# An AdaLN attention block: first row opened by halves, and no barrier between the qkv rows and the spectral products

## The reference

```python
mod = (_silu(L0_c) @ L0_wmod).reshape(L0_c.shape[0], 6, 1, -1)
sa, ca, ga, sb, cb, gb = (mod[:, 0], mod[:, 1], mod[:, 2], mod[:, 3], mod[:, 4], mod[:, 5])
...
h = _layernorm(x, axis=-1) * (1 + ca) + sa
...
q = jnp.einsum('bld,ed->bel', u, Wq) + bq[None, :, None]      # k, v alike; u is h
...
kk_f = jnp.fft.rfft(ssm_k_kernel, n=n, axis=-1)               # 512 taps for each channel
k_f = jnp.fft.rfft(k, n=n, axis=-1)
shift_k = jnp.fft.irfft(kk_f * k_f, n=n, axis=-1)[..., :l]
k = shift_k + ssm_k_D[:, None] * k
```

## Time and profile before

| | us |
|---|---|
| three runs, median | 1235.82 |
| lowest, highest | 1230.43, 1235.84 |
| the profiled execution, its own time | 1234.52 |
| its span, first to last instruction | 1232.7 |
| TensorE busy in the span | 1127.4 (91%) |
| VectorE busy | 820.3 (67%) |
| ScalarE, GpSimd busy | 420.3 (34%), 546.8 (44%) |

### The profile page before, as it was taken

The page is one execution under the profiler, slowest core; times in us unless marked ns, Lnnn a source line. Parts: engine busy times, 40 slices in busy tenths (PEclk is TensorE's granted clock), DMA queues, the critical chain, the costliest instruction groups (busy, mean ns, idle before and its releaser), DMA issues.

```text
span 1232.7 us, 16948 instructions
## 1 busy us (share of the span) xinstructions
PE 1127.4 (91%) x5744; PEld 978.5 (79%) x5744; DVE 820.3 (67%) x1543; ACT 420.3 (34%) x760; POOL 546.8 (44%) x404
## 2 busy tenths in 40 slices
PE   6899998679999999999896548999999999999996
PEld 5788887468888888888785437889898989898996
DVE  3665999679999999999656776554444445444443
ACT  3430222023333333332554212344434434344432
POOL 2330000077777777775000004476565666575623
PEclk9999999789999999999985557999999999999999
DMA  7200021154111010112431213653544444434322
GB/s 260 69 1 1 2 50 43 37 171 134 32 32 32 32 32 32 32 32 68 130 110 40 89 52 87 188 147 61 138 70 133 86 116 82 122 79 73 64 45 26
DMA packets 69361, 93.35 MB, mean 76 GB/s; under 512 B 5652, under 2 KB 57620, under 8 KB 69320
## 3 DMA queue, kind: packets, MB, share of 16 engines
q1 hardware_dynamic: 51304, 60.96, 15.6%
q0 software_dynamic: 18016, 31.86, 13.1%
HBM read 65.29 MB, written 23.31 MB: 72 GB/s over the span
## 4 chain that ended last, share of the span: by engine, by line
PE 78%; DVE 15%; issue 2%; ACT 2%; POOL 1%; DMA 1%; DVEq 0%; SPq 0%; POOLq 0%
PE ps L1305 27%; PE ps L1444 18%; PE ps L1460 12%; DVE arena L371 6%; PE ps L1461 6%; PE ps L1228 5%; PE ps L1333 2%; PE ps L1426 1%; DVE arena L1042 1%; PE ps L1354 1%; DVE arena L380 1%; PE ps L1406 1%; DVE arena L361 1%; DVE arena L362 1%; DVE arena_rounded L797 1%
## 5 line engine op out<-in xcount | busy, mean ns | idle before, releaser
L1444 PE MATMUL ps<-arena_rounded,w_high 128*128 128x384 f32 (+1 forms) x768 | 211.5, 356 | 2.1 <-DVE arena_rounded L797 2.1
L569 POOL TENSOR_TENSOR kv_low<-arena,kv_high 128x512 fp32r<-128x512 f32 x128 | 187.0, 1490 | 38.7 <-ACT kv_high L621 38.7
L1305 PE MATMUL ps<-kv_high,toep_high 128*128 128x512 f32 (+1 forms) x512 | 193.9, 379 | 11.1 <-POOL kv_low L569 11.1
L1305 PE MATMUL ps<-kv_low,toep_high 128*128 128x512 f32 (+1 forms) x512 | 194.0, 379 | 0.0
L1305 PE MATMUL ps<-kv_high,toep_low 128*128 128x512 f32 (+1 forms) x512 | 193.1, 377 | 0.0
L1159 DVE SCALAR_TENSOR_TENSOR hidden_low<-ps,hidden_high 128x384 fp32r<-128x384 f32 (+1 forms) x192 | 115.5, 602 | 99.6 <-ACT hidden_high L766 99.1
L593 POOL DMA_INDIRECT out<-arena x80 | 126.3, 1579 | 104.2 <-DVE arena L797 96.7
L582 POOL DMA_INDIRECT qkv<-row_scratch,arena x80 | 82.7, 1033 | 188.4 <-DVE arena L1113 162.3
L1444 PEld LDWEIGHTS ps<-arena_rounded,w_high 128*128 128x128 f32 x768 | 140.9, 190 | 13.1 <-issue 2.5
L797 DVE TENSOR_TENSOR arena<-qkv 128x512 f32 (+1 forms) x128 | 136.8, 1126 | 12.6 <-SPq L335 12.6
L766 ACT ACTIVATE hidden_high<-ps 128x384 fp32r<-128x384 f32 (+1 forms) x192 | 101.3, 528 | 126.8 <-PE ps L1444 126.8
(11 more groups left out here) (176 smaller groups left out, 1958.7 us busy)
## 6 DMA issues: line engine op xcount, KB each, us to landing
arena<-ssm_scratch SPq DMA_DIRECT2D x32, 320.0 KB, 3.2
arena<-in_u SPq DMA_DIRECT2D x8, 1024.0 KB, 6.5
qkv<-in_w SPq DMA_DIRECT2D x16, 512.0 KB, 5.0
qkv<-in_w SPq DMA_DIRECT2D x8, 1024.0 KB, 9.2
row_scratch<-qkv SPq DMA_DIRECT2D x4, 1056.0 KB, 4.6
qkv<-arena SPq DMA_DIRECT2D x16, 256.0 KB, 3.5
row_scratch<-arena SPq DMA_DIRECT2D x4, 1024.0 KB, 6.3
out<-qkv SPq DMA_DIRECT2D x4, 1024.0 KB, 9.5
```

Source lines behind the costliest of these rows:

```text
L569: nc.gpsimd.tensor_tensor(kv_parts[s][1][:, quarter], kv_flat[s][:, quarter], kv_parts[s][0][:, quarter].bitcast(F32), ALU.subtract).then_ ...
L1305: last = mm(ps[:, 4 * s + g, (lo - 2 * g) * B * 64:BANK], toep_parts[s][a][:, o * P:(o + 1) * P], kv_parts[s][x][:, src], start=n == 0 and ...
L1444: last = mm(ps[:, f % 4, 0:width], w1_parts[q][a][:, dc * F + f * P:dc * F + (f + 1) * P], xeT_parts[x][dc][:, 0:width], start=dc == 0 and ...
```

## The change

**The opening.** SP loads row 0 of x in two halves, ahead of wmod, and wmod in two pieces: the parts that row 0's layernorm needs (`wmod_a`, 512 of 1536 columns) and, last, the rest (`wmod_b`). w_qkv, the second row, and the bias now come ahead of the taps and `dft`; `idft` is loaded after the late modulation. TensorE begins with five matmuls of zeros that nobody reads; ScalarE loads the table of its square root early, by an `activation` whose result is not read. Row 0 is normalized, transposed and opened by halves: TensorE makes tile 0 of row 0 before it transposes the second half. The taps' spectrum moves behind row 0's tiles, the rest of the modulation behind row 1's. One of the two low parts of w_qkv moves from GpSimd to VectorE. VectorE's two clamps now both stand in row 2.

**No barrier behind qkv.** `stage_end(0)` is gone on all engines. `forward(0)` stands behind row 2's tiles, `forward(1)` between the halves of row 3, `forward(2)` behind row 3. VectorE's products of unit 0 lie between the evacuations of row 3, those of unit 1 partly so. For this the regions are laid out anew: the spectra of the units alternate between two buffers, folded results too (before, the odd ones had four places), and `folded_product` waits from unit 2 on for the whole inverse of unit u - 2. The first Toeplitz loads wait for the last fold instead of the last join.

Unit 0's operations now stand between the evacuations, one group after each. The diff's core:

```diff
-            for dc in range(DC):
-                sp.dma_start(wmod_sb[dc], wmod[dc * P:(dc + 1) * P, :]).then_inc(wmod_in, 16)
-            sp.dma_start(x_buf[0], u_tiles[0]).then_inc(x_in[0], 16)
+            sp.dma_start(x_buf[0][:, 0:TB // 2], u_tiles[0][:, 0:TB // 2]).then_inc(x_half_in, 16)
+            sp.dma_start(x_buf[0][:, TB // 2:TB], u_tiles[0][:, TB // 2:TB]).then_inc(x_in[0], 16)
+            wmod_rows = wmod.rearrange("(c p) n -> p c n", p=P)
+            sp.dma_start(wmod_a, wmod_rows[:, :, 0:2 * D]).then_inc(wmod_in, 16)
             sp.dma_start(ident[:], K["ident"]).then_inc(ident_in, 16)
+            sp.dma_start(wqkvT, w_qkv.rearrange("(c p) n -> p c n", p=P)).then_inc(w_qkv_in, 16)
...
-                if unit >= 2 and parity == 0:
-
-
-                    dve.wait_ge(conv_psum, CT * (unit - 2) + CT // 2)
...
+            if unit >= 2:
+
+
+                dve.wait_ge(conv_psum, CT * (unit - 1))
...
-            for b in range(B):
+            for b in range(B - 1):
                 qkv_out(b)
                 if b + 2 < B:
                     finish_stats(b + 2)
+                if b == 1:
+                    taps_joined()
             dve.sem_inc(mod_ready, 1)
-            stage_end(dve, 0)
...
+            qkv_rows(B - 1, 0)
+            joined_spectrum(dve, link, 0)
+            qkv_rows(B - 1, 1)
+            turned_half(link)
+            qkv_rows(B - 1, 2)
+            real_products(link, 0)
+            qkv_rows(B - 1, 3)
+            real_difference(link)
+            imaginary_products(link, 0)
+            imaginary_sum(link)
+            folded_product(dve, link, 0)
+            qkv_rows(B - 1, 4)
+            qkv_rows(B - 1, 5)
+            joined_spectrum(dve, link, 1)
+            qkv_rows(B - 1, 6)
+            turned_half(link)
+            qkv_rows(B - 1, 7)
+            real_products(link, 1)
...
+            pe.wait_ge(idle_set, 1)
+            for _ in range(5):
+                mm(ps[:, 7, :], idle[:, 0:P], idle, start=True, stop=True)
             pe.wait_ge(siluT_ready, 1)
...
+            modulation_columns(0, wmod_a, SA * D)
+            modulation_columns(2, wmod_a, CA * D).then_inc(modT_psum, 1)
...
+            def late_modulation():
+                pe.wait_ge(wmod_late_in, 16)
+                pe.wait_ge(h_full_ready, 12)
+                modulation_columns(1, wmod_b, (SB - GA) * D)
+                modulation_columns(3, wmod_b, (CB - GA) * D).then_inc(modT_psum, 1)
...
             def forward(unit):
                 b = unit // 2
+                pe.wait_ge(qkv_ready, TB * (b + 1))
+                pe.wait_ge(h_full_ready, 4 * B)
...
-            for unit in range(3):
-                forward(unit)
+            for b in range(B):
+                if b == 0:
+                    qkv_products(0, range(1))
+                    h_transposes(0, (2, 3))
+                    qkv_products(0, range(1, TB // 2))
+                else:
+                    qkv_products(b, range(TB // 2))
+                if b + 1 < B:
+                    h_transposes(b + 1)
+                if b == B - 1:
+                    forward(1)
+                qkv_products(b, range(TB // 2, TB))
+                if b == 0:
+                    taps_spectrum()
+                if b == 1:
+                    late_modulation()
+                if b == B - 2:
+                    forward(0)
+            forward(2)
+
+
+            pe.wait_ge(idft_in, 16)
             for unit in range(UNITS):
                 inverse(unit)
                 if unit + 3 < UNITS:
```

More of the change, by code:

```diff
@@ L355, in columns @@
             return slice(unit % 2 * COLS, unit % 2 * COLS + COLS)
[L357 to L373, removed]
+        def join_parities(dst, src):
+            even, odd = (parity_tiles(src, o) for o in range(2))
+            nc.vector.tensor_tensor(dst[:, 0:JR // 2], even, odd, ALU.add)
+            return nc.vector.tensor_tensor(dst[:, JR // 2:JR], even, odd, ALU.subtract)
+        s_re, s_im, t0, t1 = spec[:, real], spec[:, imag], tmp[0], tmp[1]
@@ L382, in spectral_product @@
[L382 to L390, removed]
@@ L811, in finish_stats @@
                     dve.wait_ge(h_ready, b)
-                for t in range(TB):
+                first = TB // 2 if b == 0 else 0
+                for t in range(first, TB):
                     last = nc.vector.bn_aggr(mean_var[:, t, :], stats[:, t, :])
@@ L854, in qkv_out @@
+                    qkv_rows(b, t)
+                    if b + 2 < B and t >= TB // 2:
+                        if t == TB // 2:
                             dve.wait_ge(x_in[b % 2], 16 * (b // 2 + 2))
-                        last = tile_stats(b + 2, t)
+                        for i in range(2):
+                            last = tile_stats(b + 2, 2 * (t - TB // 2) + i)
                 if b + 2 < B:
                     link(last)
+            nc.vector.memset(idle, 0.0).then_inc(idle_set, 1)
@@ new lines, in taps_spectrum @@
+            def taps_spectrum():
+                pe.wait_ge(dft_in, 16)
+                pe.wait_ge(kkT_ready, 1)
+                pe.wait_ge(h_full_ready, 8)
+                for j in range(JP):
+                    for parity in range(2):
+                        for c in range(parity, CT, 2):
+                            last = mm(ps[:, j, parity * D:(parity + 1) * D], dft[:, c, j * P:(j + 1) * P], kkT[:, c, :],
+                                      start=c == parity, stop=c == CT - 2 + parity)
+                    if j % 2:
+                        last.then_inc(kk_spec_psum, 1)
@@ L1206, in h_transposes @@
+            def h_transposes(b, pieces=range(4)):
+                if b == 0 and 0 in pieces:
+                    pe.wait_ge(h_half, 1)
+                else:
+                    pe.wait_ge(h_ready, b + 1)
+                if b == 2:
+                    pe.wait_ge(kk_copied, 2)
+                if b == 3:
+                    pe.wait_ge(modT_ready, 4)
+                    pe.wait_ge(mod_read, 1)
+                for g in pieces:
                     half, dc = g // 2, g % 2
```

292 lines of the change are left out of this document (172 added, 120 removed).

## The result

The changed kernel takes 1225.33 us (median of four runs, 1222.99 to 1226.67) against 1235.18 (1230.43 to 1235.84) for the kernel before on the same chip: 9.85 us less, a ratio of 0.9927 with an interval of 0.991 to 0.9944. The whole interval is more than 0.5% under no change: faster, as forecast, and 0.7 us from the forecast of 1226. The profiled execution took 1222.99, with a span of 1221.2.

A forecast was written before the change was run, and what follows sets the result against it. VectorE's spectral products, closely followed by TensorE, were taken to bound the stage's end. Unit 7 folded 10.55 us earlier plus a 0.8 allowance gave -9.75: 1224.8 from the profiled time, stated as 1226 us, range 1219.5 to 1232.

The forecast's parts named there:

- The opening: Start to row 3: first qkv product at 16.5 us instead of 32.92, row 3's start at 93.7 instead of 94.28.
- Rival (d): Opening: warm-up passes stay at 0.85, first product at 18 or later, 1.0 to 1.5 us; chance within the forecast's 0.6.
- rival (a): Opening's clock goes wrong: columns 3.5, whole 1.55 lost at the wait, late modulation 9.0; 1231.5 us; chance 0.22.
- The opening's worth of 0.6: Row 3 begins only 0.6 us earlier, since 16 us of earlier start are given back as later work.
- The new wait and its allowance: TensorE waits 2.45 us before row 1's transposes; 0.8, half of 1.55, allowed for a clock fall behind it.
- rival (b): Opening goes better: tile 0 at full clock (-1.55), no clock fall at the wait (-0.8); 1223.7 us; chance 0.13.
- windows at 0.50 in rows 0 to 3: Sign that would show the forecast wrong: granted clock at its lower level in the qkv rows.
- the sum: Whole change: -10.55 us for unit 7's earlier fold plus 0.8 allowance, -9.75, with the last inverse's length unchanged.
- No barrier: From row 3 on: VectorE begins unit 0 at 103.9, 17.2 us earlier, less 6.65 for seven evacuations: 10.55 earlier at unit 7.
- The rule against the change: Row 3: TensorE's short pauses for evacuations could swing its clock, running the row in part at 1.2 GHz.
- rival (c): TensorE at half clock through row 3: +6.4 us, 1242; slower only if TensorE loses over 17.7 us; chance 0.05.
- the margin: Row 3: TensorE has 5 us over; losing 7 us there would move the stage's end at most 0.5 us.

The follow-up runs named there:

- no_warmup: The changed kernel without the five TensorE matmuls of zeros at its start; 1227.28 us, ratio 0.9934 to the kernel before.
- opening_only: The changed kernel with the barrier put back, transforms and products behind it as before, so only the opening is new; 1233.92 us, ratio 0.9991 to the kernel before.
- changed_again: The changed kernel, unaltered, run again for comparison on another experiment's chip; 1226.02 us, ratio 0.9917 to the kernel before.
- more_tensor: The changed kernel with forward(1) made twice within row 3; 1232.57 us, ratio 0.9984 to the kernel before.
- more_late: The changed kernel with inverse(4) made twice, extra TensorE work ahead of the last inverses; 1223.29 us, ratio 0.9896 to the kernel before.
- gpsimd_beside: The changed kernel plus two GpSimd subtractions of 512 elements per unit on an unused region, beside VectorE's folds; 1236.86 us, ratio 1.0015 to the kernel before.

## Why the prediction was right, point by point

**The bound.** Right: VectorE's products set the end, TensorE runs 7 us short of them. In the trace unit 0 to unit 7 takes 211.11 - 104.23 = 106.88, against 106.71 forecast (seven units of 14.29, seven evacuations).

**The opening.** Warm-up passes done at 8.17 (forecast 8.8); they became faster while they ran, as assumed, and no_warmup shows that they are the cause of the faster columns: 1.92 (forecast 1.9, and 3.5 without). Rival (d) fell with that. But "left the clock low", said of the old columns, is no reading of the granted clock, whose rows give 1.00 from 8 to 30 us of the trace before; that the columns were slow there is read from their length alone, 6.96/32 = 0.22 a pass against 1.92/16 = 0.12 now. First product at 16.92, 0.4 late: GpSimd's two low quarters, the first of them beside VectorE's low part of w_qkv, took 3.20 instead of 2 x 1.29, and I had not counted what the two engines do to each other. Tile 0 and the transposes behind it ran at half clock and took 4.18 + 1.71 in the chain (forecast 3.68 + 0.95), and VectorE's tile 1 at 25.02 came ahead of `finish_stats(1)`. So row 1's transposes stood at 31.43, 1.5 late. 1.1 of it came back: the waits for evacuations in rows 1 and 2 (38.05 and 64.66) were 0.43 and 0.87, where each was 1.21 in the trace before. Late modulation took 5.3 (5.3; from 68.97 to the next tile at 74.27), not rival (a)'s 9.0. The forward transform came at 94.08 (93.7). The opening's worth of 0.6 can't be told from nothing: the last two tiles of row 2 begin at 90.02 before the change and, with this opening and its warm-up passes, at 89.30 to 90.24 in the nine executions that have this opening unchanged. That opening_only's last inverse is 0.63 earlier agrees by luck, since that gain arises at the barrier.

**The new wait and its allowance.** The wait was 2.25 (2.45), and in the profiled execution the clock stayed at 1.00, so the 0.8 was not needed; this half of rival (b) came true, its other half, tile 0 at full clock, did not. One execution misleads here: ten of the profiled ones have this wait, and only this one and no_warmup's stayed at 1.00. In the eight others the clock fell. In changed_again, the same kernel, it is 1.00 from 31 to 32 us and 0.50 from 33 to 35:

```profile
30.92 2.59 PE L1340 MATMUL ps<-ident_sb,arena 128*128 128x128 f32 x16 [2.25 <-ACT arena L642]
```

From these transposes to the forward transform it takes 94.49 - 30.92 = 63.57 there, and 94.08 - 31.43 = 62.65 where the clock stayed: 0.9 for the fall, near the 0.8 that was allowed. Of the signs of being wrong, "windows at 0.50 in rows 0 to 3" came (tile 0 of row 0); the sum itself had tile 0 at half clock, so that sign contradicted it and proves nothing.

**No barrier.** Unit 0 at 104.23 (103.9); last inverse 10.06 earlier (10.55), 8.98 long. Most of the 0.5 between them is the forward transform's delay of 0.4. TensorE's waits in row 3 were 0.81 and 0.77 (1.6), and its transforms ended at 216.81 (218.4). The span is 11.5 shorter; 10.23 of that lies ahead of the last inverse's end, and the other 1.3 in the untouched rest, less than the 3.7 by which runs of this kernel differ. That the sum (-9.75) and the medians (-9.85) are 0.1 apart is therefore partly luck: the opening was a little late, the allowance was not spent in this execution, and 1.3 comes from a part that the sum leaves out.

**The rule against the change.** The trace spoke against rival (c), and so it came: the granted clock is 1.00 from 108 to 110 and from 122 to 124 us, where TensorE waits for VectorE's evacuations. The swing between the two clock levels that the Trainium skill describes in "TensorE: Matmul & The Clock Gate", section "A second HAM failure mode: psum-queue depth-cycling", does not show in these rows.

**The step that failed** is the margin: "even if TensorE lost 7 us in row 3, the end would stay within 0.5 us". I took TensorE's slack at the last inverse for that at every point. In more_tensor 6.38 of 6.91 arrive as VectorE's waits. It didn't harm the forecast, since TensorE lost nothing in row 3, but rival (c) was priced too low by it: a loss between row 3's halves costs after 0.5 us, not after 5, and by more_tensor's rate (some 7 us for 6.91; an estimate) the gain would be gone at about 10 us lost, not at 17.7. And the sum took the last inverse's half clock as given, where more_late shows 2.7 us to be had.

**What stays open.** VectorE's waits of 0.53 at 106.7 and 0.51 at 199.5 follow joins and have no releaser that I can name; they were not tried. Why the clock fell behind the wait of 2.25 in eight executions and not in two isn't shown. The new order with the old opening was not run, so whether the order needs anything of the opening isn't shown either.

## What to carry to other kernels

When work moves across a barrier, look at which engine has something to do while the other makes what it needs: here the kernel with TensorE's new order was 10 us faster with VectorE's products between the evacuations and 6 slower without. Slack is a number at one point of the program: 5 to 7 us at the end of the stage were 0.5 us at the sixth tile of row 3. And where an engine waits long ahead of the last step of a stage, work that fills its idle time can shorten that step, and giving a part of the bounding engine's work to an idle one can lengthen it.

## What the runs showed of the hardware

**VectorE and GpSimd hold each other up.** Additions of 512 float32 elements between SBUF operands take VectorE 689 ns alone and 1778 ns beside GpSimd's, whose own take 1492 ns there, and 1286 ns for another subtraction of that size in the earlier trace rows. Two and two together took 3.54 us (118.24 to 121.78); one after the other they would be, as an estimate from these rows, 2.57 + 1.29 = 3.86. So some 0.3 us is won by doing them at once. The Trainium skill, "SBUF — State Buffer", section "Who interferes with whom", says that a VectorE instruction with two SBUF inputs contends with a GpSimd instruction that reads SBUF. The trace agrees: in unit 0 of gpsimd_beside VectorE lost 3.02 - 1.29 = 1.73 us while GpSimd worked 2.49, and over all units 1.5 us where GpSimd worked 2 x 1421 ns, about half.

**More work can be faster.** 6.9 us of TensorE work that nobody needs, put into idle time, took 2.7 us off the kernel, by the clock of the 7 us of work that followed.

**The same wait came out both ways.** Behind 2.25 us of waiting TensorE's granted clock stayed at 1.00 in two executions and fell to 0.50 in eight, the same kernel among both; the fall took 0.9 us. The wait of 2.94 before the change was followed by 0.50. A reading of the clock from one trace is a reading of one execution.
